# Destination order stored without gaps in a graph network kernel: 782 gathers per pass into a ring of 64 chunks, columns picked by loaded places

## What is computed

```python
edge_index = jnp.stack([src, dst])
x = _layernorm(x + _L0_gnn_ref(x, edge_index, edge_weight, L0_gnn_weights))   # three hops: z = segment_sum(w * z[dst], src)
x = _layernorm(x + _L1_gnn_ref(x, ...))   # relational attention, 8 heads, softmax over the edges of a destination
x = _layernorm(x + _L2_gnn_ref(x, ...))   # additive attention, 4 heads, softmax over the edges of a destination
x = _layernorm(x + _L3_gnn_ref(x, ...))   # dot attention, 8 heads, softmax over the edges of a source,
                                          # then a weighted sum over the edges of a destination
```

## Time and profile before

| | |
|---|---|
| median of 3 runs | 9734.77 us (9732.94 to 9736.07) |
| the profiled execution | 9737.26 us, span 9735.5 us |
| gathers and scatters of chunks issued by GpSimd | 1568 scatters, 5632 gathers |
| mean granted TensorE clock | 0.686 of full speed |
| relation pass, first to last gather | 5188.4 to 6251.5 us |
| left-table pass | 6429.9 to 7481.0 us |
| key pass | 7609.1 to 8591.2 us |
| weighing pass | 8636.6 to 9679.0 us |

### The profile page before, as it was taken

How to read it: one execution, slowest core, us unless ns; L and a number is a source line. 1 busy time by engine, 2 the same in 40 slices (tenths; PEclk the granted TensorE clock), 3 DMA queues, 4 the chain that set the end, 5 groups by cost and what they waited for, 6 DMA issues and landing times. The chain is left out here.

```text
span 9735.5 us, 171552 instructions
## 1 busy us (share of the span) xinstructions
PE 6374.2 (65%) x37681; PEld 5551.4 (57%) x37682; DVE 6539.5 (67%) x22695; ACT 2118.1 (22%) x6216; POOL 6993.0 (72%) x7418
## 2 busy tenths in 40 slices
PE   6777655547666577639404666767776688876666
PEld 5666544436655566634204666556675578766665
DVE  7555566668777777736305888877777666667777
...
GB/s 25 2 2 2 18 53 52 53 61 53 53 53 55 57 53 53 53 77 146 100 2 86 104 104 104 87 47 55 55 55 55 100 54 54 54 72 108 108 108 97
DMA packets 436037, 614.74 MB, mean 63 GB/s; under 512 B 176561, under 2 KB 312069, under 8 KB 435109
## 3 DMA queue, kind: packets, MB, share of 16 engines
...
## 5 line engine op out<-in xcount | busy, mean ns | idle before, releaser
L1179 PE MATMUL hop_sums<-hop_rows,hop_weighted 128*128 x4992 | 1152.1, 403 | 1053.2 <-SPq L1315 674.4
L1128 POOL DMA_INDIRECT hop_rows<-hops,k_src_gather x1568 | 1483.3, 946 | 486.8 <-issue 477.6
L1179 PEld LDWEIGHTS hop_sums<-hop_rows,hop_weighted 128*128 128x128 f32 x4992 | 989.6, 295 | 1158.8 <-issue 1158.7
L1505 POOL DMA_INDIRECT l_pass_rows<-left_table,k_dst_other x832 | 796.2, 957 | 433.2 <-issue 244.6
L1505 POOL DMA_INDIRECT l_pass_rows<-related,k_dst_typed x832 | 788.6, 948 | 308.6 <-issue 238.7
L1505 POOL DMA_INDIRECT l_pass_rows<-key_table,k_src_gather x784 | 744.3, 949 | 365.9 <-issue 234.8
L2000 POOL DMA_INDIRECT l_weigh_rows<-row_table,l_weigh_ring x832 | 790.0, 949 | 297.9 <-issue 213.1
L728 POOL DMA_INDIRECT src_sorted<-src_scatter_records,src_scatter_places x784 | 753.1, 961 | 260.4 <-issue 188.2
L1355 POOL DMA_INDIRECT dst_sorted<-rec,dst_places x768 | 752.8, 980 | 237.2 <-issue 237.2
L1128 POOL DMA_INDIRECT hop_rows<-in_x,k_src_gather x784 | 742.4, 947 | 249.0 <-issue 238.7
L1213 DVE TENSOR_SCALAR hop_weighted<-k_numbers,k_src_place,src_weight 128x128 f32<-128x128 f32 x2496 | 850.1, 403 | 15.7 <-issue 8.7
...
## 6 DMA issues: line engine op xcount, KB each, us to landing
...
hop_rows<-hops,k_src_gather POOLq DMA_INDIRECT x1568
l_pass_rows<-related,k_dst_typed POOLq DMA_INDIRECT x832
l_pass_rows<-left_table,k_dst_other POOLq DMA_INDIRECT x832
l_weigh_rows<-row_table,l_weigh_ring POOLq DMA_INDIRECT x832
src_sorted<-src_scatter_records,src_scatter_places POOLq DMA_INDIRECT x784, 2.1
hop_rows<-in_x,k_src_gather POOLq DMA_INDIRECT x784, 2.5
dst_sorted<-rec,dst_places POOLq DMA_INDIRECT x784
```

The source lines that it names most:

```text
L1128: nc.gpsimd.indirect_dma_start(rows[:, s * G + g, :], None, table_in, bass.IndirectOffsetOnAxis(ap=o.gather[:, c:c + 1], axis=0),).then_in ...
L1179: last = nc.tensor.matmul(sums[:, b, g, :], weighted[:, s % SLOTS, g, :], rows[:, bass.ds(slots[g], 1), :], start=True, stop=True)
L1505: nc.gpsimd.indirect_dma_start(rows[:, s, g, :], None, table, bass.IndirectOffsetOnAxis(ap=index[:, c:c + 1], axis=0),).then_inc(got[s], 16)
```

## The change

The destination order is stored as the source order is: without gaps, so that 100000 edges fill 782 chunks (`CHUNKS`). `place_edges` takes the place of `place_blocks` for both orders, and a new `read_lists` the place of `read_order`: it turns the two index lists by chunk, counts the readers of each group of chunks, and picks place and begin of each of the 832 columns by two one-hot products. All gather passes, those by source too, issue 782 gathers for 784 or 832, into a ring of 16 groups. In all of them SP's queue raises `landed` for each group, and then, when the group `held_back` groups ago has been read by all its columns, `freed`, on which GpSimd waits. The compute still runs over 208 groups of 4 columns. Where it read the gathered rows of a group in one instruction, it now reads them chunk by chunk, each at a place loaded into a register: VectorE's product in the relation pass, its weighted copy in the relation and left-table passes, TensorE's added row and ScalarE's copy in the left-table pass, and three VectorE instructions in the weighing pass. There the ScalarE copies of the indices go. The free counts are stored without the offset that the hops need, which SP adds.

Constants, and SP in `hop`:

```diff
-assert TU * QU == CU and RING * G == 64 and NBLK < (RING - 2) * G
+CHUNKS = -(-E // P)
+assert TU * QU == CU and 0 < CHUNKS - (GU - 1) * G <= G and RING * G == 64 and NBLK < (RING - 2) * G
...
-                    reader = sp.value_load(o.free[:, n - RING // 2:n - RING // 2 + 1], min_val=SLOTS + 1, max_val=GROUPS + SLOTS)
-                    sp.wait_ge(summed, reader)
+                    reader = sp.value_load(o.free[:, n - RING // 2:n - RING // 2 + 1], min_val=1, max_val=GROUPS)
+                    sp.wait_ge(summed, reader + SLOTS)
```

TensorE in the new `read_lists` (cut):

```diff
+        @block.tensor
+        def _(pe):
+            pe.wait_ge(counted, 2)
+            for h in range(2):
+                last = nc.tensor.transpose(readers_row[:, h * P:(h + 1) * P], readers[:, h:h + 1].to_broadcast([P, P]), k.ident[:])
+            last.then_inc(counted_row, 1)
...
+            pe.wait_ge(chosen_ok, 1)
+            pick_columns(nc, picked, zero, lambda q: by_edge[:, q, :, 0], chosen).then_inc(picked_ok, 1)
+            pe.wait_ge(found, 2)
+            pe.wait_ge(taken, 1)
+            pick_columns(nc, picked, zero, lambda q: starts[:, q, :], chosen).then_inc(picked_ok, 1)
+            pe.wait_ge(taken, 3)
+            for q in range(QT):
+                last = nc.tensor.transpose(begins_t[:, q // 4, q % 4 * P:(q % 4 + 1) * P], o.begins[:, q * TQ:(q + 1) * TQ],
+                                           k.identb[:])
+            last.then_inc(begins_ok, 1)
```

`softmax_pass`, in this order SP, GpSimd, ScalarE, TensorE, VectorE:

```diff
-            for n in range(GU if ringed else 0):
-                sp.wait_ge(got[n % RING], (n // RING + 1) * 16 * G)
+            for n in range(GU):
+                sp.wait_ge(got[n % RING], n // RING * 16 * G + 16 * min(G, CHUNKS - n * G))
                 sp.sem_inc(landed, 1)
+                if n >= held_back and n + RING - held_back < GU:
+
+                    reader = sp.value_load(o.free[:, n - held_back:n - held_back + 1], min_val=1, max_val=GROUPS)
+                    sp.wait_ge(weighed if at else scored, reader)
+                    sp.sem_inc(freed, 1)
...
-            for n in range(GU if ringed else GROUPS):
-                s = n % ring
-                if n >= ring:
-
-                    pool.wait_ge(weighed if at else scored, n - ring + 1 + (NBLK // G if ringed else 0))
+            for n in range(GU):
+                s = n % RING
+                if n >= RING:
+
+                    pool.wait_ge(freed, n - RING + 1)
                     pool.sem_inc(running, 1)
-                for g in range(G):
+                for g in range(min(G, CHUNKS - n * G)):
                     c = n * G + g
-                    nc.gpsimd.indirect_dma_start(rows[:, s, g, :], None, table,
+                    nc.gpsimd.indirect_dma_start(rows[:, s * G + g, :], None, table,
                                                  bass.IndirectOffsetOnAxis(ap=index[:, c:c + 1], axis=0),
                                                  ).then_inc(got[s], 16)
...
+                    slots_of = load_blocks(nc, act.engine, o.slot[:, t * G:(t + 1) * G], G, RING * G - 1)
                     act.wait_ge(spread_ok, t + 1)
                     if t >= 2:
                         act.wait_ge(scored, t - 1)
-                    nc.scalar.copy(pair[:, t % 2, :, :, head:deep].rearrange("p g h a -> p g (h a)"),
-                                   rows[:, t % ring, :, D:D + heads]).then_inc(joined, 1)
+                    for g in range(G):
+                        last = nc.scalar.copy(pair[:, t % 2, g:g + 1, :, head:deep].rearrange("p g h a -> p g (h a)"),
+                                              rows[:, bass.ds(slots_of[g], 1), D:D + heads])
+                    last.then_inc(joined, 1)
...
+                    if att is not None:
+                        slots_of = load_blocks(nc, pe.engine, o.slot[:, t * G:(t + 1) * G], G, RING * G - 1)
+                        need = pe.value_load(o.need[:, t:t + 1], min_val=1, max_val=GU)
...
                     if att is not None:
-                        pe.wait_ge(got[t % ring], (t // ring + 1) * 16 * G)
+                        pe.wait_ge(landed, need)
                     for g in range(G):
                         last = nc.tensor.matmul(own[:, b, g, :], onehot_t[:, b, g, :], spread[:, bass.ds(blocks[g], 1), :],
                                                 start=True, stop=(att is None))
                         if att is not None:
-                            last = nc.tensor.matmul(own[:, b, g, :], k.ident[:], rows[:, t % ring, g, 0:D],
+                            last = nc.tensor.matmul(own[:, b, g, :], k.ident[:], rows[:, bass.ds(slots_of[g], 1), 0:D],
                                                     start=False, stop=True)
                     last.then_inc(spread_ok, 1)
...
-                    if ringed:
+                    if att is None:
                         slots_of = load_blocks(nc, dve.engine, o.slot[:, t * G:(t + 1) * G], G, RING * G - 1)
                         need = dve.value_load(o.need[:, t:t + 1], min_val=1, max_val=GU)
                         dve.wait_ge(landed, need)
-                    else:
-                        dve.wait_ge(got[t % ring], (t // ring + 1) * 16 * G)
                     dve.wait_ge(spread_ok, t + 1)
                     if t >= 2:
                         dve.wait_ge(scored, t - 1)
-                    if ringed:
-                        by_chunk = rows[:].rearrange("p r g f -> p (r g) f")
+                    if att is None:
                         for g in range(G):
                             last = nc.vector.tensor_tensor(pair[:, b, g:g + 1, :, :].rearrange("p g h f -> p g (h f)"),
-                                                           own[:, b, g:g + 1, :], by_chunk[:, bass.ds(slots_of[g], 1), :],
+                                                           own[:, b, g:g + 1, :], rows[:, bass.ds(slots_of[g], 1), 0:D],
                                                            ALU.mult)
                         last.then_inc(paired, 1)
-                    elif att is None:
-                        nc.vector.tensor_tensor(pair[:, b, :, :, :].rearrange("p g h f -> p g (h f)"), own[:, b, :, :],
-                                                rows[:, t % ring, :, 0:D], ALU.mult).then_inc(paired, 1)
                     else:
...
-                    nc.vector.tensor_tensor(
-                        terms[:, m % 2, :, 0:D].rearrange("p g (h f) -> p g h f", h=heads),
-                        rows[:, m % ring, :, values_at:values_at + D].rearrange("p g (h f) -> p g h f", h=heads),
-                        held[:, c:c + G, :].rearrange("p g (h a) -> p g h a", a=1)
-                        .to_broadcast([P, G, heads, head]), ALU.mult).then_inc(weighed, 1)
+                    slots_of = load_blocks(nc, dve.engine, o.slot[:, m * G:(m + 1) * G], G, RING * G - 1)
+                    for g in range(G):
+                        last = nc.vector.tensor_tensor(
+                            terms[:, m % 2, g:g + 1, 0:D].rearrange("p g (h f) -> p g h f", h=heads),
+                            rows[:, bass.ds(slots_of[g], 1), values_at:values_at + D].rearrange("p g (h f) -> p g h f", h=heads),
+                            held[:, c + g:c + g + 1, :].rearrange("p g (h a) -> p g h a", a=1)
+                            .to_broadcast([P, 1, heads, head]), ALU.mult)
+                    last.then_inc(weighed, 1)
```

`weigh_and_sum`, ScalarE, GpSimd, SP, VectorE:

```diff
-                    list_rows(n + SLOTS - 1, (s + SLOTS - 1) % SLOTS)
...
-            with pool.Fori(0, ROUNDS) as i:
-                for s in range(SLOTS):
-
-                    pool.wait_ge(listed, i * SLOTS + s + 1)
+            for n in range(GU):
+                s = n % RING
+                if n >= RING:
+
+                    pool.wait_ge(freed, n - RING + 1)
                     pool.sem_inc(running, 1)
-                    for g in range(G):
-                        nc.gpsimd.indirect_dma_start(rows[:, s, g, :], None, table,
-                                                     bass.IndirectOffsetOnAxis(ap=ring[:, s, g:g + 1], axis=0),
-                                                     ).then_inc(got[s], 16)
+                for g in range(min(G, CHUNKS - n * G)):
+                    c = n * G + g
+                    nc.gpsimd.indirect_dma_start(rows[:, s * G + g, :], None, table,
+                                                 bass.IndirectOffsetOnAxis(ap=index[:, c:c + 1], axis=0),
+                                                 ).then_inc(got[s], 16)
+
+        @block.sync
+        def _(sp):
+            for n in range(GU):
+                sp.wait_ge(got[n % RING], n // RING * 16 * G + 16 * min(G, CHUNKS - n * G))
+                sp.sem_inc(landed, 1)
+                if n >= 8 and n + RING - 8 < GU:
+
+                    reader = sp.value_load(o.free[:, n - 8:n - 7], min_val=1, max_val=GROUPS)
+                    sp.wait_ge(weighed, reader + SLOTS)
+                    sp.sem_inc(freed, 1)
...
```

(35 more changed lines are left out.)

334 lines of the change are left out of this document (144 added, 190 removed).

## The result

The changed kernel takes 10465.49 us (median of 4 runs, 10460.95 to 10472.55) against 9733.85 (9729.43 to 9736.07) on the same chip: ratio 1.0754, 95% interval 1.0740 to 1.0768. The forecast had the sign and a third of the size. The profiled execution has a span of 10458.8 us (9735.5 before).

What follows compares the result with a forecast made beforehand. VectorE's in-order chain was taken to bound the relation pass, GpSimd's gathers the other three. Relation pass +229, late start +15, left-table -45, weighing +20, key pass and hops -10, preparing +11 gave +220: 9955 us, range 9760 to 10150.

Steps and rivals of the forecast that it cites:

- Relation pass, loads: VectorE's register loads per window of 4 groups: 0.97 and 0.82 us before products, 0.7 and 0.45 before weighted copies.
- Relation pass, splits: VectorE's product and weighted copy in four pieces each: 0.63 and 0.84 us, together 1.47 per window of 4 groups.
- Late start and ring: Relation pass: SP announces rows only behind its loads of the breaks, so compute starts later; +15 us, between 0 and +52.
- Rival D: Announcements or freed places come late, left-table pass stays at 1051 and the ring is no help: about 10010 us, chance 0.03.
- Weighing pass: VectorE's added loads, splits and subtractions lift its floor from 3.69 to 5.1 us per group: +20 us, bounds -62 and +95.
- Key pass: Two gathers fewer with compute untouched: -10 us together with the hops, -2 for the key stage.
- Left-table pass: 50 gathers fewer, added work fits inside TensorE's wait for rows: -45 us, bounds -62 and +10.
- Start: From the start to the relation pass: +3 us, with +11 for preparing, where two column picks stand in a row.
- Rival B: Loads are hidden in all passes and only the splits count: 9715 us, about even, chance 0.13.
- Rival C: TensorE's clock falls too, +90 us in the relation pass, up to 75 in the weighing pass: 10050 to 10120, chance 0.18.
- signs named for being right: Profile signs: VectorE period near 24.9 us, issue gaps 0.8 to 1.0, GpSimd waiting for freed places, 782 gathers, pass times.

Runs made afterwards that it cites:

- the fifth run: The changed kernel with all lists that VectorE loads from on the first partition, in all four passes: 10242.82 us.
- Eased: The changed kernel with loads issued early, lists on one partition and TensorE instead of VectorE waiting for need: 9815.91 us, ratio to before 1.0083.

## Why the prediction was wrong

The bound was read rightly: VectorE's in-order chain sets the relation pass, and GpSimd's saving fell into its shadow. The step that failed is the price of VectorE's register loads: 2.94 us per relation window, 0.7 per weighing group, nothing in the key pass. The runs showed 4.8 us of idle time and 6.0 us of window, 1.6 us of idle time per group, and +64 us.

- **Relation pass, loads** ("the add (0.71) and the mark (0.68) cover them: 0"). First, the place of the lists: the price was taken from a pass whose lists lay on one partition. With the lists there (the fifth run), the idle time before products is 55.7 us for 120 groups, 1.86 per window, beside a forecast of 0.97 + 0.82 = 1.79; the 0.20 to 0.22 behind the mark is gone, so the cover had been read rightly for that case. With the lists apart it is 2.7. Second, the adds' own loads were left out: 1.0 us per window, of which 0.34 are left with the lists on one partition. They show only where the copies' places are loaded before them: behind four pieces at fixed places the adds wait 0.1 us in 800. The copies' loads were priced at 1.15 and took 1.0. Third, that idle time isn't all: with loaded places the window is 6.0 us longer than with the same pieces at fixed ones. Where the rest lies was not tried apart.
- **Relation pass, splits** (1.47). In pieces alone 1.5 us of busy time and 0.8 of window. With early loads the window is 2.0 us longer (22.4 - 20.48) although the gaps are gone, so 1.1 us of that remain unexplained.
- **Late start and ring** (+15): 30 against the old buffer. Within its bounds. Rival D falls too: with ring and SP as they are the left-table pass gains 41 us once the lists lie side by side.
- **Weighing pass** (5.1 us per group: 0.5 for the product's loads, 0.2 for the add's, 0.48 for splits, 0.2 for subtractions). Measured per group: 1.05 before the product and 0.5 before the mark for the loads, and the rest mostly in pieces and subtractions, 6.4 in all. Of the loads 0.4 is the place of the lists (6.0 us per group and 1300.9 for the stage in the fifth run). The upper bound (+95) doubled the small pieces but never the loads. Eased, the group takes 5.1 us and the stage is +23.
- **Key pass** ("Their compute is untouched"): its instructions were, its lists were moved. I priced the gathers and not the place of the lists. +64, of which the run with lists side by side gives back 47.
- **Left-table pass** (-45): +7, for the same reason; -41 with the lists side by side.
- **Start** (+3): -12. From the load of the destination list to the first gather it took 22.6 us before and 30.7 after, +8 where +11 was forecast. The work ahead of it ended 20 us earlier, where the forecast had 8; why was not looked into.
- **Rival B** is half right: with the loads issued early 140 us of idle time became 7, so a load under long work leaves no gap. But where each load stands decides, and here most stood bare. The Trainium skill's "Perfetto Trace Analysis", section "Sequencer Loop", says that a sequencer pushes engine instructions into a queue and reads on; the trace agrees, with those 7 us.
- **Rival C**: the granted clock fell, from 0.82 to 0.71 in the relation pass and from 0.72 to 0.54 in the weighing pass. The time of the changed kernel didn't come from there: TensorE's three answers cost 2.8 us per window instead of 3.5, and in the weighing pass VectorE's gaps are "issue". Where the gaps shrink at a low clock, as in the fifth run, the answers take more (3.7).

Of the signs named for being right, issue gaps before the products, GpSimd waiting for places and 782 gathers were there. The period on VectorE was 27.3 us for 24.9. From first to last gather, the relation pass took 1385 us for 1250 to 1350, the left-table pass 1042 for 1005 and the weighing pass 1241 for 1060.
